# Attention by four heads at once, in column tiles of 32, with denominators from GpSimd's sums

## The reference, cut to what matters

```python
q = concat_e( xn_e[:, :m_e] @ q_w[:, :m_e].T + q_b )   # 4096 x 256; k and v alike
q, k, v -> 8 heads of 32
attn = softmax(q @ k.T * 256**-0.5)                    # 4096 x 4096 for each head
attn_out = attn @ v                                    # then o_w by slices, + o_b, + x
```

## Time and profile before

| | us |
|---|---|
| median of 3 runs (4659.76 to 4662.38) | 4660.43 |
| the profiled execution | 4664.79 |
| its span | 4663.0 |
| from the start of the second norm's loads (2377.8) to the attention's (2679.2) | 301.4 |
| first maxima of the attention (2692.0) to first scores (2743.2) | 51.2 |
| first scores to the start of the last scores (4635.2) | 1892.0 |
| from there to the end of the span | 27.8 |

### The profile page before, as it was taken

The page is one execution under the profiler, slowest core; times in us unless marked ns, Lnnn a source line. Parts: engine busy times, 40 slices in busy tenths (PEclk is TensorE's granted clock), DMA queues, the critical chain, the costliest instruction groups (busy, mean ns, idle before and its releaser), DMA issues. The chain is left out here.

```text
span 4663.0 us, 151762 instructions
## 1 busy us (share of the span) xinstructions
PE 4392.9 (94%) x64527; PEld 2836.3 (61%) x64527; DVE 3304.3 (71%) x5496; ACT 1912.8 (41%) x2685; POOL 1037.3 (22%) x1042
## 2 busy tenths in 40 slices
PE   4999799999999999999968789999999999999998
PEld 3444489999999999996756624444444444444443
DVE  5799765565555655553459778787878888887876
ACT  2888411111111111110434426565655556565654
POOL 1000144344344344341047630000000000000000
PEclk9999899999999999999989979999999999999999
DMA  3534411111111111112344330000000000000000
GB/s 117 180 115 136 140 56 51 55 56 54 52 56 54 53 56 54 52 47 68 115 123 110 98 72 9 9 14 9 13 9 13 9 13 9 13 9 13 9 13 9
DMA packets 261650, 250.10 MB, mean 54 GB/s; under 512 B 51712, under 2 KB 230016, under 8 KB 260256
## 3 DMA queue, kind: packets, MB, share of 16 engines
q1 hardware_dynamic: 240528, 209.39, 15.0%
q0 software_dynamic: 6144, 16.79, 1.1%
q10 hardware_dynamic: 14352, 14.55, 0.9%
HBM read 135.27 MB, written 105.38 MB: 52 GB/s over the span
## 5 line engine op out<-in xcount | busy, mean ns | idle before, releaser
L2204 DVE TENSOR_REDUCE part_max<-p_m 128x1 f32<-128x512 f32 x2118 | 1364.0, 686 | 380.9 <-PE p_m L2046 373.4
L2186 ACT ACTIVATE prob<-p_s 128x1024 f32<-128x1024 f32 x1024 | 1047.7, 1023 | 750.8 <-PE p_s L2110 748.8
L2065 PE MATMUL p_o<-prob,v_one 128*64 128x512 f32 x4096 | 1054.4, 593 | 3.9 <-ACT prob L2186 0.5
L2046 PE MATMUL p_m<-keys,queries 96*64 96x512 f16 x4236 | 660.9, 387 | 28.7 <-DMA keys<-parts_d 21.1
L2110 PE MATMUL p_s<-queries,keys 97*64 97x512 f16 x4096 | 618.8, 380 | 0.2 <-issue 0.2
L2110 PEld LDWEIGHTS p_s<-queries,keys 97*64 97x64 f16 x4096 | 226.5, 109 | 601.7 <-issue 596.0
L2046 PEld LDWEIGHTS p_m<-keys,queries 96*64 96x64 f16 x4236 | 238.2, 108 | 313.5 <-DVE part_max L2204 56.5
L831 PE MATMUL pd_pre<-inv,step 64*64 64x64 f32 x10240 | 385.1, 219 | 24.6 <-issue 22.9
L2014 POOL TENSOR_TENSOR attn<-o_num,o_inv 32x512 f32<-32x512 f32 x64 | 81.0, 1266 | 1453.9 <-DVE o_inv L2223 1447.4
L2065 PEld LDWEIGHTS p_o<-prob,v_one 128*64 128x64 f32 x4096 | 286.3, 136 | 163.5 <-issue 16.1
L831 PEld LDWEIGHTS pd_pre<-inv,step 64*64 64x64 f32 x10240 | 345.9, 135 | 57.5 <-issue 55.8
(11 more groups left out here) (245 smaller groups left out, 6619.4 us busy)
## 6 DMA issues: line engine op xcount, KB each, us to landing
q_d<-conv_q SPq DMA_DIRECT2D x16, 1024.0 KB, 5.0
v_d<-conv_v SPq DMA_DIRECT2D x16, 1024.0 KB, 5.0
k_d<-conv_k SPq DMA_DIRECT2D x16, 1024.0 KB, 6.5
sums<-sums_d SPq DMA_DIRECT2D x128, 128.0 KB, 3.0
k_t<-k_d SPq DMA_DIRECT2D x32, 512.0 KB, 4.5
q_t<-q_d SPq DMA_DIRECT2D x32, 512.0 KB, 3.4
v_t<-v_d SPq DMA_DIRECT2D x32, 512.0 KB, 3.4
slots_d<-zero ACTq DMA_DIRECT2D x1, 10112.0 KB, 31.2
```

The lines of the kernel that those rows point to most:

```text
L2046: last = te.matmul(p_m[k % 2][x * HALF:(x + 1) * HALF, :], queries[0:ROW, p, hh, at:at + HALF], keys[0:ROW, 2 * p + hh, kb * BLK:(kb + 1) ...
L2065: product = te.matmul(p_o[64 * hh:64 * hh + VW, :], g.v_one[:, j, p, hh:hh + 2, :].rearrange("p a d -> p (a d)"), prob[:, j % 2, hh, :], s ...
L2186: a.activation(prob[:, j % 2], p_s[j % 2][:], ACT.Exp, scale=SCORE_SCALE).then_inc(exp_d, 1)
L2204: v.tensor_reduce(part_max[:, hh * SUB + sub, kb:kb + 1], p_m[k % 2][:], AX.X, ALU.max).then_inc(red_d, 1)
```

## The change

Four heads are done at once: 16 groups in place of 32, with 64 steps s each. Step s takes tile j = s // 2 and the pair r = s % 2 of the four heads. All loops are written out; before, the 8 blocks were one copy for the first and a loop over seven.

- Scores: 8 products of 32 columns in place of 4 of 64, four beside each other in the array.
- Maxima: a group has 128 numbers. They are made at steps 4 to 60 of the group before, 2, 3, 1 and 3 in every four steps, each as four products of 32 columns. One goes ahead of the values, the others behind. All 128 numbers of group 0 come before the first scores.
- Values: at every odd step, for one key tile and four heads; 4 products of 32 columns, without ones.
- Denominators: POOL adds the probabilities of an odd tile to those of the even tile before it, a pair of heads at a time (128 x 1024). Every fourth step PE multiplies the sum with 32 columns of ones, into its own bank `p_d`. `prob` has 4 buffers in place of 2.
- ACT takes numerators and denominators out of PSUM and copies 4 maximum rows for each group. DVE inverts in place. POOL has one multiplication of 128 x 512 for each group in place of four of 32 x 512 (two groups before).
- The products that used `p_f` use `p_m` now, outside the steps that make maxima.
- The second norm writes values without ones (`g.v_all`), and the fill is 32 columns (`g.ones_v`) in place of 12288.

```diff
-        po.memset(g.v_one[:], 1.0).then_inc(cleared, 1)
+        po.memset(g.ones_v[:], 1.0).then_inc(cleared, 1)
...
+    FIRST_MAX, LAST_MAX = 4, 60
+    PER_STEP = (2, 3, 1, 3)
+    INVERT_FROM, DENR_FROM = 10, 12
+    DENS_AT, EXTRA_AT, ROWS_AT, FINAL_AT = 3, 61, 62, 63
...
# SP
+        for b, c, n in groups():
+            if c == 0:
+                if b > 0:
+                    sp.wait_ge(nums_d, b * KC)
+                sp.dma_start(lin_q[:], ...).then_inc(lq_in, 16)
+            sp.wait_ge(s_d, (n + 1) * NS)
+            for p in (2 * c, 2 * c + 1):
                 load_queries(b + 1, p)
...
# POOL
+        def add_pairs(n, i, r):
+            pool.wait_ge(exp_d, n * NS + (2 * i + 1) * 2 + r + 1)
+            pool.wait_ge(pv_d, n * NKT + 2 * i + 1)
+            even, odd = 2 * i % 4, 2 * i % 4 + 1
+            po.tensor_tensor(prob[:, even, r], prob[:, even, r], prob[:, odd, r], ALU.add).then_inc(pair_sum_d, 1)
...
# PE
+            if n > 0 or k >= 2:
                 pe.wait_ge(red_d, n * NMAX + (k - 1))
+            for q, quarter in enumerate(QUARTERS):
+                at = sub * P + q * DF
+                last = te.matmul(p_m[k % 2][quarter, :], queries[0:ROW, p, x, at:at + DF],
+                                 keys[0:ROW, 2 * p + x, kb * BLK:(kb + 1) * BLK], start=True, stop=True)
...
+        for b, c, n in groups():
+            pe.wait_ge(rowc_d, (n + 1) * HQ)
+            for s in range(NS):
+                if s % 4 == 0:
...
+                        denominators(n, i)
...
+                scores(n, s)
...
+                numbers = max_numbers(s)
+                for k in numbers[:1]:
+                    max_product(n + 1, k)
+                if s % 2 == 1:
+                    j = (s - 3) // 2
...
+                        values(n, j)
...
+                for k in numbers[1:]:
+                    max_product(n + 1, k)
+                if s == DENS_AT and c == 0:
+                    pe.wait_ge(ready, READY)
+                    pe.wait_ge(lq_in, b * 16 + 16)
...
+                        te.matmul(p_m[x][:], ks_block[:, x, :], lin_q[:, x, :], start=True, stop=True).then_inc(dens_d, 1)
...
# ACT
+            for s in range(NS):
+                exponentials(n, s)
+                if s == 1 and n > 0:
+                    take_numerators(n - 1)
+                if s == 4 and n > 0:
+                    take_denominators(n - 1)
+                if s == ROWS_AT:
+                    copy_rows(n + 1)
...
# DVE
+                for k in max_numbers(s):
+                    max_reduce(n + 1, k)
+                if n > 0 and s >= INVERT_FROM and (s - INVERT_FROM) % 4 == 0 and (s - INVERT_FROM) // 4 < PIECES:
+                    invert(n - 1, (s - INVERT_FROM) // 4)
+                if s >= DENR_FROM and (s - DENR_FROM) % 4 == 0 and (s - DENR_FROM) // 4 < PIECES:
...
+                    v.reciprocal(piece, piece).then_inc(denr_d, 1)
```

More of the change, by code:

```diff
@@ L1855, in phase_attention @@
     KR = ROW + 1
[L1856 to L1864, removed]
+    QUARTERS = [slice(q * DF, (q + 1) * DF) for q in range(HQ)]
+    NMAX = HQ * SUB * KB
+    NSUM = NKT // 2
     PIECES = 8
@@ L1913, in phase_attention, with groups, max_numbers @@
     g.used_sems = sems
[L1915 to L1928, removed]
+    def groups():
+        for b in range(NB):
+            for c in range(KC):
+                yield b, c, b * KC + c
+    def max_numbers(s):
+        if not FIRST_MAX <= s <= LAST_MAX:
+            return range(0)
+        start = sum(PER_STEP[x % 4] for x in range(FIRST_MAX, s))
+        return range(start, min(start + PER_STEP[s % 4], NMAX))
     def max_step(k):
-        hh, rest = divmod(k, NMAX // 2)
+        hh, rest = divmod(k, NMAX // HQ)
         return (hh,) + divmod(rest, KB)
@@ L2004, in _, with normalise @@
         pool.wait_ge(ready, READY)
[L2006 to L2022, removed]
-                    pool.wait_ge(base_in, b * 16 + 16)
[L2024 to L2032, removed]
+        def add_pairs(n, i, r):
[3 more added lines that the diff above has]
+            po.tensor_tensor(prob[:, even, r], prob[:, even, r], prob[:, odd, r], ALU.add).then_inc(pair_sum_d, 1)
+        def normalise(n):
+            if n // KC > 0:
+                pool.wait_ge(fin_d, n // KC * SUB)
+            pool.wait_ge(o_d, n + 1)
+            pool.wait_ge(inv_d, (n + 1) * PIECES)
+            po.tensor_tensor(attn[:, n % KC, :], o_raw[:], o_inv[:], ALU.mult).then_inc(attn_d, 1)
+        for b, c, n in groups():
+            for i in range(NSUM):
+                for r in range(2):
+                    add_pairs(n, i, r)
+                if i == NORMALISE_AT and n > 0:
+                    normalise(n - 1)
+                if i == BIAS_AT and c == 1:
+                    pool.wait_ge(base_in, b * 16 + 16)
+                    po.tensor_tensor(base[:], base[:], spread(bias_b[:, b:b + 1, :], [P, SUB, D]), ALU.add).then_inc(bb_d, 1)
+        normalise(LAST)
     @block.tensor
@@ L2036, in _, with max_product @@
         te = nc.tensor
-        def max_product(n, p, k):
+        def max_product(n, k):
             hh, sub, kb = max_step(k)
-            if k >= 2 or not isinstance(n, int) or n > 0:
+            p, x = n % KC * 2 + hh // 2, hh % 2
+            if n > 0 or k >= 2:
                 pe.wait_ge(red_d, n * NMAX + (k - 1))
[L2044 to L2047, removed]
+            for q, quarter in enumerate(QUARTERS):
+                at = sub * P + q * DF
+                last = te.matmul(p_m[k % 2][quarter, :], queries[0:ROW, p, x, at:at + DF],
+                                 keys[0:ROW, 2 * p + x, kb * BLK:(kb + 1) * BLK], start=True, stop=True)
@@ L2070, in final, with scores @@
-        def final(b, s):
+        def scores(n, s):
+            j, r = divmod(s, 2)
+            p = n % KC * 2 + r
+            if n * NS + s > 1:
+                pe.wait_ge(exp_d, n * NS + s - 1)
+            for hh in range(2):
+                for q, quarter in enumerate(QUARTERS):
+                    at = j * P + q * DF
+                    last = te.matmul(p_s[r][quarter, hh, :], keys[0:KR, 2 * p + hh, at:at + DF], queries[0:KR, p, hh, :], start=True, stop=True)
+            last.then_inc(s_d, 1)
@@ new lines, in values, with denominators @@
+        def values(n, j):
+            if j == 0 and n > 0:
+                pe.wait_ge(o_d, n)
+            pe.wait_ge(exp_d, n * NS + 2 * j + 2)
+            for q, quarter in enumerate(QUARTERS):
+                last = te.matmul(p_o[quarter, :], g.v_all[:, j, n % KC * HQ + q, :], prob[:, j % 4, q // 2, q % 2, :],
+                                 start=j == 0, stop=j == NKT - 1)
+            last.then_inc(pv_d, 1)
+        def denominators(n, i):
+            if i == 0 and n > 0:
+                pe.wait_ge(den_d, n)
+            pe.wait_ge(pair_sum_d, (n * NSUM + i + 1) * 2)
+            for q, quarter in enumerate(QUARTERS):
+                last = te.matmul(p_d[quarter, :], g.ones_v[:], prob[:, 2 * i % 4, q // 2, q % 2, :], start=i == 0, stop=i == NSUM - 1)
+            last.then_inc(dn_d, 1)
@@ L2159, in _ @@
+        values(LAST, NKT - 1)
+        denominators(LAST, NSUM - 2)
+        denominators(LAST, NSUM - 1)
+        pe.wait_ge(rowc_d, (LAST + 2) * HQ)
         for s in range(SUB):
-            final(NB - 1, s)
+            if s > 1:
+                pe.wait_ge(out_d, (NB - 1) * SUB + s - 1)
+            final(NB - 1, s, s % 2)
     @block.scalar
@@ L2164, in _, with copy_rows @@
         a = nc.scalar
[L2166 removed]
+        def copy_rows(n):
             act.wait_ge(row_d, n + 1)
[L2168 to L2178 removed]
@@ L2180, in one @@
-        def one(b, before):
-            for p in range(HP):
-                n = b * HP + p
-                for j in range(NKT):
-                    act.wait_ge(pv_d, n * NKT + (j - 1) if before is not None or p > 0 or j > 0 else 0)
-                    act.wait_ge(s_d, n * NKT + (j + 1))
-                    a.activation(prob[:, j % 2], p_s[j % 2][:], ACT.Exp, scale=SCORE_SCALE).then_inc(exp_d, 1)
-                    if j == 1 and p > 0:
-                        take_nums(b * HP + (p - 1))
-                    elif j == 1 and before is not None:
-                        take_nums(before * HP + (HP - 1))
-                    if j == NKT - 2:
-                        copy_rows(n + 1, (p + 1) % HP)
@@ L2194, in _, with take_numerators, take_denominators @@
-        blocks(act, one)
-        take_nums(NB * HP - 1)
+            for q in range(HQ):
+                a.activation(queries[ROW:KR, n % KC * 2 + q // 2, q % 2, :], p_m[0][q * DF:q * DF + 1, :], ACT.Copy).then_inc(rowc_d, 1)
+        def take_numerators(n):
+            if n > 0:
+                act.wait_ge(attn_d, n)
+            act.wait_ge(pv_d, n * NKT + NKT)
+            a.activation(o_raw[:], p_o[:], ACT.Copy).then_inc(o_d, 1)
+        def take_denominators(n):
+            if n > 0:
+                act.wait_ge(attn_d, n)
+            act.wait_ge(dn_d, n * NSUM + NSUM)
```

(1 more changed line is left out.)

295 lines of the change are left out of this document (126 added, 169 removed).

## The result

The changed kernel takes 4677.83 us in the median of 14 runs (4672.02 to 4682.07), the kernel before 4663.83 in 14 runs beside them: ratio 1.0032, 95% interval 1.0025 to 1.0038. So it is slower by 0.3%, 14 us, and the forecast was 48. The profiled executions have spans of 4675.0 and 4663.0.

What follows compares the result with a forecast made beforehand. PE was taken to bound the kernel, with DVE at 81%. Loop +10, start +45, fill -6 and end 0 gave +49 us on 4664.79, so 4713, or 4708 against the median; own range 4665 to 4765, full range 4618 to 4830.

Steps and rivals of the forecast that it cites:

- point 1: PE's repeated work in a group of 64 steps falls from 110.5 to 96.7 us, 221 us less over 16 groups.
- The fours without reciprocals: Four loop steps with maxima but no reciprocals: 6.26 us of PE work becomes 6.95 through waits for reductions.
- the start: Before the first scores, 128 numbers take 91.3 us; first scores at 2788.2 in place of 2743.2: +45 us.
- the fill: Before the attention, DVE and the loads of x start earlier without the large fill: -6 us, least 3, most 10.
- the adds: POOL's add of 128 x 1024 in the loop takes 2.35 us and is covered up to 3.5 us.
- the end: After the last exp: 1 to 2 us later, which the finals with two banks give back: 0.
- The other eight steps of a group: Steps of a group outside 4 to 59: 14.2 us in an odd group, 20.7 in an even one.
- rival B: Much slower: four tiles are not as fast as two; sets 10% longer give 4820 us; chance 0.15.
- Rival A: Faster: waits of maxima 3, 5, 6 and 9 are shorter than laid out; 4520 us with none; chance 0.2.
- point 2: In four loop steps with maxima, PE waits for DVE's reductions; two reciprocals make a four 7.44 us, against 6.95 without.
- point 4: In step 3 of a block's first group PE waits for lin_q, 2.1 us seven times: 15 us.
- The loop's figure: Main loop, first to last scores: 1904 us against 1893.7, +10.

Runs made afterwards that it cites:

- e3: Changed kernel with the next block's lin_q load issued before the wait for the last scores and the query loads: ratio 1.0013 to the kernel before, loop 1854.9 us.
- e1: Changed kernel with each maximum reduction reading 256 of 512 columns: ratio 0.9675 to the kernel before, loop 1714.8 us.
- e8: Kernel before the change, with each maximum reduction reading 256 of 512 columns: ratio 0.9952 to the kernel before, loop 1884.9 us.
- e4: Changed kernel with the same work reordered, maxima 2, 3, 0, 4 in four steps and reciprocals moved: ratio 0.9799 to the kernel before, loop 1756.0 us.
- e2: Changed kernel with reciprocals of steps 10 to 40 on 1 column in place of 64: ratio 0.9975 to the kernel before, loop 1833.9 us.
- e6: Changed kernel with POOL adding 16 of 512 columns of each probability tile: ratio 1.0028 to the kernel before, loop 1868.1 us.
- e10: Changed kernel with only the maxima reordered (2, 3, 0, 4), reciprocals left in place: ratio 0.9871 to the kernel before, loop 1791.0 us.
- e7: Changed kernel with reordered maxima and reciprocals, early lin_q load and four banks at the start together: ratio 0.9735 to the kernel before, 4524.31 us.
- e5: Changed kernel with four PSUM banks in place of two for the maxima before the first scores: ratio 0.9998 to the kernel before, start 81.1 us.

## Why the prediction was right and wrong

**Right in kind.** The work that PE saves (221 us by point 1) doesn't arrive, because products and reductions take turns through two banks. After has 8 fours of 7.19 and 6 of 6.93 in a group against 6.26 of work: 11.5 us, and 10.0 in group 0, 182 in the loop. 221 - 182 = 39 would be left, and 26.6 were measured. The other 12 are, by difference, lost at the groups' ends; 10.5 of them are the waits for `lin_q` (e3). e1, e8 and e4 show the mechanism from three sides: shorten the reduction, do so before the change, space the products.

**Right in size.** The fours without reciprocals (6.95 against 6.93), the start (+45 against +44.0), the fill (-6 against -5.2), the adds (2.35 against 2.36), the end (0 against -0.2). The other eight steps of a group too: 14.4 us against 14.2 in an odd one, and in an even one, in e3 where `lin_q` is there, 20.3 against 20.7 (its terms as listed add up to 20.2). The tiles: rival B asked for sets more than 0.23 apart, they are 0.216. Rival A needed the waits to be gone; they are there.

**Wrong: point 2's reciprocals.** This is the step that failed, "reduction 3 is 3.47 to 4.16 and maximum 5 waits to 4.24 (0.44)" and its twin of 0.40. I put a reciprocal at its recorded 0.54 us between one reduction's 0.61 and a full 0.69 of the next. The chain has 0.46 for it, and the reduction behind it starts 0.08 before the reciprocal's recorded end and is 0.63 long, not 0.69:

```profile
3513.31 0.54 DVE L2236 RECIPROCAL o_inv<-o_inv 128x64 f32<-128x64 f32 x1
3513.77 1.95 DVE L2222 TENSOR_REDUCE part_max<-p_m 128x1 f32<-128x512 f32 x3
```

In a four of the trace, from the start of its denominators, reduction 3 is 3.40 to 4.03 and maximum 5 waits to 4.08 in place of 4.24, and maximum 9 to 6.96 in place of 7.23. Maximum 6 then starts at 4.76, where it starts without a reciprocal, so the first reciprocal is free, where the laying out had it cost 0.10. Together it is 0.25 us in a four and 2.1 in a group. By the prediction the reciprocals cost 59 us, by e2 31.5, and this makes 28 of the 36.6 us of the miss. I had the evidence in the earlier trace rows: two reductions of 0.69 that take 1.29 together overlap, and I used this for reductions only.

**Mis-sized: point 4.** `lin_q` was put at 2.1 us seven times, 15; e3 has 10.5. It landed 9.6 to 10.9 us after the start of the last scores in the seven blocks, no earlier than laid out (9.6). But PE comes to that step later than I had it: 8.4 us after the start of the last scores in five of e3's blocks, where nothing holds it there, and 9.5 in the other two, against 7.5. Another 4.5 us are the 0.02 between 6.95 and 6.93 in each of the 224 fours. 28 + 4.5 + 4.5 = 37. What else was off cancels: the first group took 114.1 us where I had 110.9, and the last was about as much shorter.

**What failed as a forecast.** The loop's figure was a difference of two sums of 1900 us. A 2% error in one of the two is 37 us, more than the effect, and the forecast's own range (4665 to 4765) was drawn from the clock and +-0.2 us a four. 4678 was inside it, yet the change was a third of the size. The way it went was not read from the loop either, where +10 turned out as -26.6; the start's +44 carried it.

## What to carry to other kernels

When an engine's work is cut, look at who hands it its buffers: with two buffers the chain product, reduction, release (here 1.20 us from a product to the next one in the same bank) must fit between every second use, wherever in the step the uses lie, and an average share of 81% doesn't show that it won't. Lay the order out in hundredths before the edit; spacing the same instructions by that rule was worth 109 us here, and the cut of work without it 27. Put side work of the second engine where it would wait anyway; there reciprocals that had cost 31 us cost none. In such a layout take each operation at its spacing in a back-to-back run, not at its recorded length.

## What the runs showed of the hardware

A small DVE conversion took seven times as long beside POOL's adds. The line of `neg_max` (ns min/median/max), after and in e6 with small adds:

```profile
L2231 DVE TENSOR_SCALAR neg_max<-row_max x17: 174/1201/1203, 2778.5 to 4644.9; 128x16 f16<-128x16 f32 x17
```

```profile
L2231 DVE TENSOR_SCALAR neg_max<-row_max 128x16 f16<-128x16 f32 x17 | 3.0, 175 | 0.6
```

1.20 us against 0.175, and 0.172 before. It reads and writes SBUF with one source; the reductions, which read PSUM, take 0.680 us on average with the large adds and with the small ones. In all 16 of the loop `neg_max` starts within an add and ends 0.03 us after that add's end. That fits the Trainium skill, SBUF — State Buffer, section SBUF: two separate sides: one port pair is shared by VectorE and GpSimd as an exclusive lock, and a VectorE operation in a mode that uses two ports waits for the GpSimd instruction that holds it to end. Not every operation from SBUF to SBUF is hit: 128 of the 248 reciprocals of 64 columns lay wholly within an add and kept their 0.54 us. The loop of e6 isn't shorter, so the wait cost nothing here.

The granted clock fell to its lower level for single stretches inside the loop, which it didn't before. Around a block's end, after (windows as above):

```profile
3472.40:3475.80 3.40, 3.33 (x43) 1.02 (x41) 1.98 (x3) 1.45 (x2) 0.75 (x1) 1.00 0.00 0
3475.80:3479.20 3.40, 1.35 (x20) 0.54 (x24) 0.00 (x0) 2.94 (x5) 2.62 (x2) 1.00 0.30 70
3479.20:3482.60 3.40, 3.40 (x32) 1.15 (x28) 0.00 (x0) 2.51 (x3) 2.08 (x1) 0.50 0.46 122
```

PE had been busy for 1.35 of 3.4 us, while it waited for the row copies, and the next 3.4 us ran at 0.50, the 1.2 GHz level. The trace of after has three such stretches in the loop, that of e10 seven. In e7 the three groups with one are 0.7 to 1.1 us longer than their like, in e5 one is 2 to 3 us longer. Every run of the changed kernel, edited or not, has at least two of them.
